# Last attention group taken by sequences, and the token masks built in the first group

## The chip, the cores and the metric

The kernel runs on 1 core of one Trainium2 chip. The metric is the device time of one execution in microseconds (us): 590.84 us, the median of 3 runs (588.93 to 592.22).

## The reference, cut to what matters

One decoder layer on x of shape 4 sequences x 256 tokens x 256 channels, all float32:

```python
x = x + attn(layernorm(x))              # 16 heads of 128, mxfp4-style codes * scales as weights
h = layernorm(x)                        # routed FFN: 4 experts, all with weights ctx[e] (256 x 256)
expert_ids = min(clip(token_ids, 0, 12499) // 3125, 3)
for e in range(4):
    g = silu(h @ ctx[e].T); u = h @ ctx[e].T
    y = (g * u) @ ctx[e].T
    out = where(expert_ids == e, y, out)
x = x + out
x = x + moe(layernorm(x))               # 32 experts, top 4 of a sigmoid router, and a shared expert
```

The masks of this case are the four tests `expert_ids == e` for 1024 tokens, as numbers 0 and 1 on all 128 partitions.

## The kernel before, in words

Tokens are 1024 = 8 row tiles of 128. Float32 products are made of three passes over a high and a low part (`mm3`, L723 to L725). The 16 heads are taken two at a time in G = 8 groups; a group has PAIRS = 8 pairs of (head of the group `hp`, sequence `b`), in the order (0,0) (0,1) (0,2) (0,3) (1,0) (1,1) (1,2) (1,3). The body of a group (`body`, run by `over_groups`: group 0, a loop for groups 1 to 6, group 7) is a software pipeline of slots. In slot i TensorE makes the scores of pair i, then a projection tile of place 0, the transposes (`turn`) of pair i-2, the product with V (`attend`) of pair i-3, and a tile of place 1. Which tiles stand where is the table `slot_tiles`: "qk" tiles of the second head, "v" tiles, "w" tiles (output projection of the group before, one for each sequence, added to the residual `x_acc` by VectorE, L1232), and "next" tiles (first head of the next group). Group 7 has no "next" tiles; its own four output projections stood in slots 8 to 11.

ScalarE does exp (L1098), the high parts of every tile (L1075, L1082), of the transposed probabilities (`pT_hi`, L1110) and of the attention output (`oT_hi`, L1119). VectorE does the row maximum (L1260), its negative (`nmax`, L1264), the scaling of the probabilities (L1273) and the low parts (L1241, L1245, L1281, L1288). Every engine works its own queue strictly in the order written.

GpSimd (POOL) prepares the weights, four chunks for each group (H0, VC, H1, WC): `prep` multiplies codes by scales (L524, counted by `p_wm`), waits until ScalarE has made the high part (`weights_high`, L1052, counted by `a_wh`), and makes the low part (L527, counted by `p_wl`). In groups 1 to 6 ScalarE makes the high part of H0 at the end of slot 1, of VC in slot 5, H1 in slot 6 and WC in slot 7, and its `wait(act, p_wm, count)` stands in its queue ahead of the exp of the next slot. `masks()` (L545 to L555) stood at the head of group 7 in the queue of GpSimd: 4 comparisons and 2 subtractions over 1024 columns. The token ids had landed in group 0. In group 0 the same queue ends with the prep of WC and `constants()`.

After group 7 comes the layer norm of the first token half (statistics, variances, square root on ScalarE, reciprocals with a Newton step, rows; L653 to L682), its transposes on TensorE (L702), high and low parts (L708, L714), then the routed FFN: 16 steps, `pre(n)` and `post(n)` on TensorE, silu on ScalarE (L1149), multiplication with the mask on GpSimd (L591) and the rest on VectorE. `pre(0)` waits for the low parts of the first half. The transposes of the second half stand behind `pre(2)`. Then follow the router and the 32 experts in 8 trips of 8 tiles.

Of the kernel before, what the change touches and what calls it, by code (L numbers as in the profile page):

```python
# [17 lines left out]
P = 128  # L18
T = 1024
# [14 lines left out]
NH = T // HALF  # L34
NE, TOPK, FI = 32, 4, 128
# [29 lines left out]

def slot_tiles(first, last):

    s = [[("qk", Q, 1, 0), ("w", W, 0, 0)],  # L70
         [("qk", K, 1, 0), ("w", W, 0, 1)],
         [("qk", Q, 1, 1), ("v", V, 0, 0)],
         [("v", V, 0, 1), ("w", W, 0, 2)],
         [("v", V, 0, 2), ("qk", K, 1, 1)],
         [("v", V, 0, 3), ("w", W, 0, 3)],
         [("next", Q, 0, 0), ("next", K, 0, 0)],
         [("next", Q, 0, 1), ("next", K, 0, 1)]]
    def tile(t):
        if first and t[0] == "w":
            return ("ctx", None, 0, t[3])  # L80
        return None if last and t[0] == "next" else t
    return [[tile(t) for t in slot] for slot in s]
# [10 lines left out]
class Plan:  # L93
# [3 lines left out]
    def __init__(self, g):  # L97
        self.g = g
        self.first = isinstance(g, int) and g == 0
        self.last = isinstance(g, int) and g == G - 1  # L100
        self.slots = slot_tiles(self.first, self.last)
        n = 0
        self.tiles = []
        start = 4 + 16 * g
        for i, slot in enumerate(self.slots):
            for place, t in enumerate(slot):
                if t is not None:
                    self.tiles.append((i, t, start + n, n, place))
                    n += 1
        if self.last:  # L110
            for b in range(B):
                self.tiles.append((PAIRS + b, ("w", W, 0, b), start + n, n, 1))
                n += 1

    def of_slot(self, i, place):
        if i < 0:
            return [] if self.first else [(("prev", K, 0, 1), None, 1, False)]
        return [(t, number, pos, s >= PAIRS) for s, t, number, pos, at in self.tiles if s == i and at == place]
# [21 lines left out]
    def freed(self, pos):  # L140

        if pos >= 2:
            t = self.tiles[pos - 2][1]
            final = self.last and self.tiles[pos - 2][0] >= PAIRS
        else:
            t, final = ("prev", (Q, K)[pos], 0, 1), False
        kind, m, hp, n = t
        if kind in ("prev", "qk", "next"):
            return "qk", self.qk_count(t)
        if kind == "v":  # L150
            return "v", self.v_count(n)
        if kind == "ctx":
            return "ctx", n + 1
        return "w", self.w_done_count(n, final)

    def w_tile_number(self, b):

        for s, t, number, pos, place in self.tiles:
            if t[0] == "w" and t[3] == b and s < PAIRS:
# [18 lines left out]
def decoder_layer(nc, a, out):  # L178
    ctx = ExitStack()
    with ctx:  # L180
# [78 lines left out]
        mask = sb("mask", [P, NROUTE, T])  # L259
# [252 lines left out]
        def _(pool):  # L512
# [16 lines left out]
            for n, nm in enumerate(("bq", "bk", "bv")):  # L529
# [5 lines left out]
                               base=0, pattern=[[-1, P]], channel_multiplier=1).then_inc(p_const, 1)  # L535
            for n, c in enumerate((H0, H1, VC)):
# [9 lines left out]
            def masks():  # L546
# [3 lines left out]
                for e in range(NROUTE):  # L550
                    pool.tensor_scalar(mask[:, e, :], ids[:, :], float(per * e) if e else float(per), None,
                                       ALU.is_ge if e else ALU.is_lt).then_inc(p_mask, 1)
                pool.wait_ge(p_mask, NROUTE)
                for e in range(1, NROUTE - 1):
                    pool.tensor_tensor(mask[:, e, :], mask[:, e, :], mask[:, e + 1, :], ALU.subtract).then_inc(p_mask, 1)  # L555
# [16 lines left out]
            def body(pl):  # L572
                g = pl.g
                if pl.last:
                    masks()
                for c in ((WC,) if pl.last else (H0, VC, H1, WC)):
# [4 lines left out]
                    if pl.first and c == WC:  # L581
                        constants()

# [3 lines left out]
            pool.wait_ge(p_mask, 2 * NROUTE - 2)  # L587
# [132 lines left out]
        def _(pe):  # L720
# [14 lines left out]
            def proj_tile(pl, tile, number, pos, final=False):  # L735
# [31 lines left out]
                else:  # L767
# [3 lines left out]
                    wait(pe, v_o, pl.pair(PAIRS if final else 0) - B + n + 1)  # L771
# [9 lines left out]
            def scores(pl, i):  # L781
                p = pl.pair(i)
                wait(pe, a_exp, p - 1 if not (pl.first and i < 2) else 0)
                hp, b = i // B, i % B
# [20 lines left out]
            def attend(pl, i):  # L805
# [4 lines left out]
                hp, b = (i % PAIRS) // B, i % B  # L810
                if 0 <= i < B:
# [13 lines left out]
            def body(pl):  # L825
                for i in range(PAIRS + (DRAIN + 1 if pl.last else 0)):
# [45 lines left out]
            ln_tensor(pe, 1, 0, ENDS[0])  # L872
# [173 lines left out]
        def _(act):  # L1046
# [44 lines left out]
            def body(pl):  # L1091
                for i in range(PAIRS + (DRAIN + 1 if pl.last else 0)):
# [18 lines left out]
                    if not (pl.first and i < ATTEND) and i < PAIRS + ATTEND:  # L1111
                        j = i - ATTEND
                        hp, b = (j % PAIRS) // B, j % B
# [10 lines left out]
                    if (i in prep_slots and not pl.last) or (i == PAIRS - 2 and pl.last):  # L1124
# [4 lines left out]
                        elif c != WC or not pl.first:  # L1129
                            kind = {VC: "v", H1: "qk", WC: "w"}[c]  # L1130
                            wait(act, t_j, [tile[2] for tile in pl.tiles if tile[1][0] == kind and tile[0] < PAIRS][-1] + 1)
                        weights_high(c, pl.weights(c, 0 if c == WC else 1))

            over_groups(act, body)

            ln_scalar(act, 1, 0)
# [72 lines left out]
        def _(dve):  # L1209
# [45 lines left out]
            def body(pl):  # L1255
                for i in range(PAIRS + (DRAIN + 2 if pl.last else 0)):
# [26 lines left out]
                    if not (pl.first and i < ATTEND) and i < PAIRS + ATTEND:  # L1283
                        j = i - ATTEND
                        hp, b = (j % PAIRS) // B, j % B
# [4 lines left out]
                                                 op0=ALU.add, op1=ALU.subtract).then_inc(v_o, 1)  # L1290
                    if pl.last and i == PAIRS + 2:
# [8 lines left out]
            ln_low(dve, 1, 0, ENDS[0])  # L1300
# [185 lines left out]
```

## Time and profile before

| what | value |
|---|---|
| median of the runs shown | 590.84 us |
| profiled execution | 591.11 us, span 589.4 us |
| granted TensorE clock, mean of the span | 0.935 |
| PE busy | 511.3 us (87%) |
| DVE busy | 426.6 us (72%) |
| ACT busy | 288.2 us (49%) |
| POOL busy | 233.5 us (40%) |

Attention fills the span from about 28 us to 348 us, the routed FFN the stretch from 354 to about 406 us, the router and the experts the rest. PE, DVE, ACT and POOL are TensorE, VectorE, ScalarE and GpSimd. One group in the loop takes 38.92 us.

### The profile page before, as it was taken

To read this page: it belongs to the slowest core of one execution; us is meant where nothing else is said; L and a number is where in the kernel's file an instruction comes from. 1 tells how busy PE (TensorE), PEld (TensorE's weight loads), DVE (VectorE), ACT (ScalarE), POOL (GpSimd) and SP (SyncE) were. 2 spreads that over 40 slices of the span, in tenths; PEclk is the share of its full clock that TensorE was granted. 3 is DMA by queue.
4 is the path that set the end of the run, shared out by engine and by line. 5 is a ranking of instruction groups with operands and counts; after the bars stand their busy time and mean duration, and the time that the engine had idled before them with its cause. 6 is when DMAs were issued, how large, how long until landed. Compare 5 with 4: busy or idle time off the path is not lost.

```text
span 589.4 us, 11588 instructions
## 1 busy us (share of the span) xinstructions
PE 511.3 (87%) x3291; PEld 453.0 (77%) x3292; DVE 426.6 (72%) x967; ACT 288.2 (49%) x785; POOL 233.5 (40%) x221
## 2 busy tenths in 40 slices
PE   5899999999999999999997679997837999999800
PEld 5688898998998989989887677886625888888600
DVE  5689988989889888898899776568685444444542
ACT  2466656556666666566654625444400444444400
POOL 4307413313123042131384004445005666777773
PEclk9789999999999999999999888999875999999955
DMA  7252211202102122020072009991101455423642
GB/s 214 65 138 55 63 29 51 65 1 83 32 27 62 27 53 62 14 75 0 0 237 86 2 2 296 296 264 37 36 2 35 136 156 147 134 82 112 193 135 89
DMA packets 60893, 52.91 MB, mean 90 GB/s; under 512 B 5545, under 2 KB 58623, under 8 KB 60800
## 3 DMA queue, kind: packets, MB, share of 16 engines
q1 hardware_dynamic: 55752, 43.90, 25.3%
q0 software_dynamic: 4704, 8.44, 5.8%
q8 instruction: 16, 0.26, 0.2%
q10 hardware_dynamic: 408, 0.20, 0.1%
q14 instruction: 13, 0.11, 0.1%
HBM read 46.21 MB, written 14.68 MB: 103 GB/s over the span
## 4 chain that ended last, share of the span: by engine, by line
PE 54%; DVE 19%; issue 9%; POOL 9%; ACT 4%; DMA 3%; POOLq 1%; DVEq 0%; ACTq 0%
PE bank L723 14%; PE bank L724 13%; PE bank L725 13%; PE bank L893 5%; POOL yg L639 5%; POOL xg_last L628 3%; DVE qk_lo L1245 3%; PE bank L801 3%; DVE rmax L1260 3%; DVE nmax L1264 3%; PE bank L901 2%; ACT qk_hi L1082 2%; DMA x_in<-in_x 2%; ACT prob L1098 1%; DVE pT_lo L1281 1%
## 5 line engine op out<-in xcount | busy, mean ns | idle before, releaser
L527 POOL TENSOR_TENSOR w_lo<-st_c,w_hi 128x512 fp32r<-128x512 f32 x32 | 41.2, 1287 | 220.7 <-ACT w_hi L1052 220.7
L1098 ACT ACTIVATE prob<-bank,nmax 128x256 f32<-128x256 f32 x128 | 59.5, 470 | 111.2 <-DVE nmax L1264 111.2
L893 PE MATMUL bank<-moe_w,xT 128*128 x256 | 67.6, 388 | 0.0
L723 PE MATMUL bank<-hT_hi,w_lo 128*128 128x512 f32 x128 | 53.9, 421 | 7.8 <-DVE qk_lo L1245 4.2
L1340 DVE TENSOR_TENSOR hid<-bank,sg 128x128 f32<-128x128 f32 x72 | 20.9, 291 | 53.4 <-ACT sg L1164 52.7
L1245 DVE SCALAR_TENSOR_TENSOR qk_lo<-bank,b_col,qk_hi 128x512 fp32r<-128x512 f32 x64 | 47.8, 747 | 13.2 <-ACT qk_hi L1082 12.2
L1260 DVE TENSOR_REDUCE rmax<-bank 128x2 f32<-128x512 f32 x64 | 43.9, 686 | 15.8 <-PE bank L725 15.2
L1164 ACT ACTIVATE sg<-bank 128x128 f32<-128x128 f32 x72 | 19.8, 277 | 70.0 <-PE bank L893 69.9
L1273 DVE TENSOR_SCALAR prob<-prob,rinv 128x256 f32<-128x256 f32 x128 | 52.0, 448 | 2.3
L724 PE MATMUL bank<-hT_lo,w_hi 128*128 128x512 f32 x128 | 51.6, 403 | 0.0
L725 PE MATMUL bank<-hT_hi,w_hi 128*128 128x512 f32 x128 | 51.4, 402 | 0.0
L1082 ACT ACTIVATE qk_hi<-bank,b_col 128x512 fp32r<-128x512 f32 x64 | 44.0, 687 | 10.8 <-PE bank L725 10.0
L893 PEld LDWEIGHTS bank<-moe_w,xT 128*128 128x128 f32 x256 | 44.8, 195 | 3.6
L1281 DVE TENSOR_TENSOR pT_lo<-bank,pT_hi 128x512 fp32r<-128x512 f32 x64 | 43.6, 681 | 3.1 <-ACT pT_hi L1110 3.1
L723 PE MATMUL bank<-pT_hi,v_lo 128*128 128x256 f32 x128 | 41.8, 326 | 4.0 <-DVE pT_lo L1281 2.7
L524 POOL TENSOR_TENSOR st_c<-st_c,st_s 128x512 f32<-128x512 f32 x32 | 40.9, 1279 | 5.5 <-DMA st_s<-in_wq_scales 5.5
L801 PE MATMUL bank<-ident,prob 128*128 128x128 f32 x256 | 38.6, 274 | 1.8 <-DVE prob L1273 1.8
L723 PE MATMUL bank<-w_hi,oT_lo 128*128 128x256 f32 x128 | 37.4, 292 | 2.4 <-DVE qk_lo L1245 2.4
L1110 ACT CAST pT_hi<-bank 128x512 fp32r<-128x512 f32 x64 | 38.1, 595 | 2.6 <-PE bank L801 2.6
L591 POOL TENSOR_TENSOR x_in<-x_in,mask 128x512 f32<-128x512 f32 x16 | 20.9, 1306 | 45.0 <-ACT x_in L1149 45.0
L901 PE MATMUL bank<-moe_w,hidT 128*128 x128 | 38.3, 382 | 0.0
L723 PE MATMUL bank<-w_hi,hT_lo 128*128 128x256 f32 x128 | 36.3, 283 | 2.0 <-DVE qk_lo L1245 2.0
(187 smaller groups left out, 1609.0 us busy)
## 6 DMA issues: line engine op xcount, KB each, us to landing
y_dram<-ysb SPq DMA_DIRECT2D x64, 128.0 KB, 2.4
moe_w<-in_w_gate SPq DMA_DIRECT2D x8, 512.0 KB, 8.5
moe_w<-in_w_up SPq DMA_DIRECT2D x8, 512.0 KB, 7.2
moe_w<-in_w_down SPq DMA_DIRECT2D x4, 1024.0 KB, 8.8
st_c<-in_wq_codes SPq DMA_DIRECT2D x16, 128.0 KB
st_c<-in_wv_codes SPq DMA_DIRECT2D x8, 256.0 KB
st_c<-in_wo_codes SPq DMA_DIRECT2D x8, 256.0 KB
st_s<-in_wo_scales SPq DMA_DIRECT2D x16, 128.0 KB
```

The costliest lines, as they stand in the source:

```text
L723: pe.matmul(o, l_lo, r_hi, start=start, stop=False, skip_group_check=share)
L724: pe.matmul(o, l_hi, r_lo, start=False, stop=False, skip_group_check=share)
L725: return pe.matmul(o, l_hi, r_hi, start=False, stop=stop, skip_group_check=share)
L801: mm = pe.transpose(bP[i % 2][:, kt * S + qt * P:kt * S + qt * P + P], prob[:, i % 4, qt, kt * P:kt * P + P], ident[:, :])
L893: mm = pe.matmul(bG[n % 2][:, 0:2 * FI], xT_of(kt), w, start=kt == 0, stop=kt == KT - 1)
L901: pe.matmul(bY[n % 2][:, 0:D], hidT[:, n % 2, :], w, start=True, stop=True).then_inc(t_dn, 1)
L1082: act.activation(qk_hi[:, hp, m, n * HALF:(n + 1) * HALF], src[:, :], ACT.Identity, bias=b_col[:, bass.ds(g_h + m * H, 1)]).then_inc(a_qk, 1)
L1098: ex = act.activation(prob[:, i % 4, qt, :], bS[i % 2][:, qt * S:(qt + 1) * S], ACT.Exp, bias=nmax[:, i % 2, qt:qt + 1], scale=SCALE, accu ...
L1245: dve.scalar_tensor_tensor(out=qk_lo[:, hp, m, n * HALF:(n + 1) * HALF], in0=src[:, :], scalar=b_col[:, bass.ds(g_h + m * H, 1)], in1=qk_h ...
L1260: dve.tensor_reduce(rmax[:, i % 2, :], bS[i % 2][:, :].rearrange("p (q k) -> p q k", q=2), AX.X, ALU.max).then_inc(v_m1, 1)
L1273: sc = dve.tensor_scalar(prob[:, j % 4, qt, :], prob[:, j % 4, qt, :], rinv[:, j % 2, qt:qt + 1], None, ALU.mult)
L1281: dve.tensor_tensor(pT_lo[:, j % 2, :, :].rearrange("p a b -> p (a b)"), bP[j % 2][:, :], pT_hi[:, j % 2, :, :].rearrange("p a b -> p (a b ...
```

## The change

Four edits. In group 7 the pairs are taken in the order of `LAST_ORDER`; the tiles stand in other slots, with the output projections of sequences 0 and 1 in slots 6 and 7 and those of 2 and 3 in slots 10 and 11; the high part of the last WC chunk is made in slot 5 instead of 6. The layer norm of the first half is spread over slots 8 to 11, its transposes standing ahead of the last output projection. The masks are bf16, built in pieces of 256 columns (16 comparisons, 8 subtractions) behind `constants()` in group 0. A tile `beyond` of 4096 bf16 columns is added behind `mask` and cleared by GpSimd ahead of its first `prep`.

```diff
+LAST_ORDER = [(0, 0), (0, 1), (1, 0), (1, 1), (0, 2), (0, 3), (1, 2), (1, 3)]
 def slot_tiles(first, last):
+    if last:
+        return [[("qk", Q, 1, 0), ("w", W, 0, 0)],
+                [("qk", K, 1, 0), ("w", W, 0, 1)],
+                [("qk", Q, 1, 1), ("v", V, 0, 0)],
+                [("v", V, 0, 1), ("w", W, 0, 2)],
+                [("qk", K, 1, 1), ("w", W, 0, 3)],
+                [("v", V, 0, 2), None],
+                [("v", V, 0, 3), ("w", W, 1, 0)],
+                [None, ("w", W, 1, 1)]]
...
-            for b in range(B):
-                self.tiles.append((PAIRS + b, ("w", W, 0, b), start + n, n, 1))
+            for i, b in ((PAIRS + 2, 2), (PAIRS + 3, 3)):
+                self.tiles.append((i, ("w", W, 1, b), start + n, n, 1))
...
-        mask = sb("mask", [P, NROUTE, T])
+        mask = sb("mask", [P, NROUTE, T], BF16)
+        beyond = sb("beyond", [P, NROUTE, T], BF16)
...
+            pool.memset(beyond[:, :, :], 0.0)
             for n, c in enumerate((H0, H1, VC)):
                 prep(c, n + 1, 16 * DMAS[c])
...
+                for i in range(MASK_PIECES):
+                    sl = slice(i * S, (i + 1) * S)
+                    for e in range(NROUTE):
+                        pool.tensor_scalar(mask[:, e, sl], ids[:, sl], float(per * e) if e else float(per), None,
+                                           ALU.is_ge if e else ALU.is_lt).then_inc(p_mask, 1)
+                    pool.wait_ge(p_mask, i * MASK_STEPS + NROUTE)
+                    for e in range(1, NROUTE - 1):
+                        pool.tensor_tensor(mask[:, e, sl], mask[:, e, sl], mask[:, e + 1, sl], ALU.subtract).then_inc(p_mask, 1)
...
             def body(pl):
                 g = pl.g
-                if pl.last:
-                    masks()
...
                     if pl.first and c == WC:
                         constants()
+                        masks()
...
# TensorE, slots of the last group
+                    if pl.last and i == PAIRS + 3:
+                        ln_tensor(pe, 1, 0, ENDS[0])
                     for tile in pl.of_slot(i, 1):
                         proj_tile(pl, *tile)
...
# ScalarE
-                    if (i in prep_slots and not pl.last) or (i == PAIRS - 2 and pl.last):
+                    if (i in prep_slots and not pl.last) or (i == PAIRS - 3 and pl.last):
...
+                    if pl.last and i == PAIRS + 1:
+                        ln_scalar(act, 1, 0)
...
# VectorE
+                    if pl.last and i == PAIRS:
+                        dve.wait_ge(v_w, 4 * G - 1)
+                        statistics()
+                    if pl.last and i == PAIRS + 1:
+                        variances()
                     if pl.last and i == PAIRS + 2:
-                        dve.wait_ge(v_w, 4 * G - 1)
-                        for part in ln_vector(dve, 1, 0, x_acc):
-                            part()
+                        reciprocals()
+                        rows()
+                    if pl.last and i == PAIRS + 3:
+                        ln_low(dve, 1, 0, ENDS[0])
```

## Rows read from the trace of the kernel before

**Rows 1.** The page: the clock granted to TensorE in 40 slices, in tenths.
```profile
PEclk9789999999999999999999888999875999999955
```

**Rows 2.** Busy time by stretch: stretch, its us, each engine, granted clock, DMA share, GB/s.
```profile
298.00:318.00 20.00, 16.45 (x122) 15.08 (x121) 19.36 (x33) 9.69 (x29) 17.66 (x8) 1.00 0.69 237
```

**Rows 3.** The tile mask, instructions that write it: count, ns min/median/max, starts, forms.
```profile
L551 POOL TENSOR_SCALAR mask<-ids x4: 2770/2774/2799, 298.7 to 307.2; 128x1024 f32<-128x1024 int32 x4
L555 POOL TENSOR_TENSOR mask<-mask x2: 2373/2404/2435, 310.1 to 312.4; 128x1024 f32<-128x1024 f32 x2
```

**Rows 4.** Timeline of DVE, group 7: start us, us, instruction.
```profile
309.00 3.62 DVE L1273 TENSOR_SCALAR prob<-prob,rinv 128x256 f32<-128x256 f32 x2
...
316.80 0.62 DVE L1273 TENSOR_SCALAR prob<-prob,rinv 128x256 f32<-128x256 f32 x2
```

**Rows 5.** Timeline of PE: first matmul of slots 0 and 5, groups 6 and 7.
```profile
256.74 0.28 PE L723 MATMUL bank<-qk_hi,qk_lo 128*128 128x256 f32 x1
...
280.90 0.28 PE L723 MATMUL bank<-qk_hi,qk_lo 128*128 128x256 f32 x1
...
295.67 0.28 PE L723 MATMUL bank<-qk_hi,qk_lo 128*128 128x256 f32 x1
...
323.76 0.28 PE L723 MATMUL bank<-qk_hi,qk_lo 128*128 128x256 f32 x1
```

**Rows 6.** Timeline of POOL, start of the program and groups 0 and 1.
```profile
3.05 0.23 POOL L531 MEMSET ident<- 128x128 f32 x1
...
3.63 0.29 POOL L534 TENSOR_SCALAR_AFFINE_SELECT ident<-ident 128x128 f32<-128x128 f32 x1 [0.24 <-POOL zeros L532]
9.41 1.28 POOL L524 TENSOR_TENSOR st_c<-st_c,st_s 128x512 f32<-128x512 f32 x1 [5.49 <-DMA st_s<-in_wq_scales]
...
44.63 5.71 POOL L543 TENSOR_TENSOR x_acc<-x_in,bo_b 128x256 f32<-128x256 f32 x8
...
65.37 0.29 POOL L567 TENSOR_SCALAR_AFFINE_SELECT before<-ones 128x128 bf16<-128x128 bf16 x1
...
65.90 1.28 POOL L524 TENSOR_TENSOR st_c<-st_c,st_s 128x512 f32<-128x512 f32 x1
```

**Rows 7.** Timeline of ACT, group 1, end of slot 1 and slot 2.
```profile
72.14 0.64 ACT L1052 CAST w_hi<-st_c 128x512 fp32r<-128x512 f32 x1
74.28 0.47 ACT L1098 ACTIVATE prob<-bank,nmax 128x256 f32<-128x256 f32 x1 [1.50 <-DVE nmax L1264]
...
75.19 0.69 ACT L1082 ACTIVATE qk_hi<-bank,b_col 128x512 fp32r<-128x512 f32 x1
```

**Rows 8.** Timeline of PE, group 1, slot 3: first v matmul, and the turn behind it.
```profile
77.55 0.28 PE L723 MATMUL bank<-w_hi,hT_lo 128*128 128x256 f32 x1
...
78.97 0.60 PE L801 MATMUL bank<-ident,prob 128*128 128x128 f32 x4
```

**Rows 9.** Timeline of PE, group 7, slots 8 and 9, and routed stage.
```profile
337.97 0.58 PE L723 MATMUL bank<-pT_hi,v_lo 128*128 128x256 f32 x1 [2.38 <-DVE pT_lo L1281]
...
341.98 0.79 PE L801 MATMUL bank<-ident,prob 128*128 128x128 f32 x4
...
353.76 0.80 PE L723 MATMUL bank<-hT_hi,cT_lo 128*128 128x512 f32 x1 [1.75 <-DVE hT_lo L714]
```

**Rows 10.** Timeline of ACT and then of DVE, end of group 7.
```profile
335.23 1.28 ACT L694 ACT_TABLE_LOAD   x1
...
346.24 0.48 DVE L1288 SCALAR_TENSOR_TENSOR oT_lo<-bank,b_col,oT_hi 128x256 fp32r<-128x256 f32 x1 [0.60 <-ACT oT_hi L1119]
346.64 1.40 DVE L653 BATCH_NORM_STATS2 bn<-x_acc 128x6 f32<-128x256 f32 x4
...
348.79 0.18 DVE L665 RECIPROCAL rstd<-sd 128x4 f32<-128x4 f32 x1 [0.27 <-ACT sd L690]
...
349.80 1.38 DVE L682 TENSOR_SCALAR h_row<-x_acc,mv,rstd 128x256 f32<-128x256 f32 x4
351.10 1.28 DVE L1232 TENSOR_TENSOR x_acc<-bank,x_acc 128x512 f32<-128x512 f32 x2
```

More of the change, by code:

```diff
@@ L34 @@
 NH = T // HALF
+MASK_PIECES, MASK_STEPS = T // S, 2 * 4 - 2
 NE, TOPK, FI = 32, 4, 128
@@ L80, in tile @@
             return ("ctx", None, 0, t[3])
-        return None if last and t[0] == "next" else t
+        return t
     return [[tile(t) for t in slot] for slot in s]
@@ L110, in __init__, with pair_of @@
         if self.last:
-            for b in range(B):
-                self.tiles.append((PAIRS + b, ("w", W, 0, b), start + n, n, 1))
+            for i, b in ((PAIRS + 2, 2), (PAIRS + 3, 3)):
+                self.tiles.append((i, ("w", W, 1, b), start + n, n, 1))
                 n += 1
+    def pair_of(self, i):
+        if self.last and 0 <= i < PAIRS:
+            return LAST_ORDER[i]
+        return i % PAIRS // B, i % B
     def of_slot(self, i, place):
@@ L117, in of_slot @@
             return [] if self.first else [(("prev", K, 0, 1), None, 1, False)]
-        return [(t, number, pos, s >= PAIRS) for s, t, number, pos, at in self.tiles if s == i and at == place]
+        return [(t, number, pos, t[0] == "w" and t[2] == 1) for s, t, number, pos, at in self.tiles if s == i and at == place]
     def pair(self, i):
@@ L143, in freed @@
             t = self.tiles[pos - 2][1]
-            final = self.last and self.tiles[pos - 2][0] >= PAIRS
+            final = t[0] == "w" and t[2] == 1
         else:
@@ L158, in w_tile_number @@
         for s, t, number, pos, place in self.tiles:
-            if t[0] == "w" and t[3] == b and s < PAIRS:
+            if t[0] == "w" and t[3] == b and t[2] == 0:
                 return number
@@ L770, in proj_tile @@
                         wait(pe, p_wl, pl.weights(WC, 0) if final else (pl.g - 1) * 4 + 3 + 4)
-                    wait(pe, v_o, pl.pair(PAIRS if final else 0) - B + n + 1)
+                    wait(pe, v_o, pl.pair(LAST_ORDER.index((1, n)) if final else n - B) + 1)
                     for i in range(2):
@@ L809, in attend @@
                 wait(pe, v_o, p - 1 if not (pl.first and 0 <= i < 2) else 0)
-                hp, b = (i % PAIRS) // B, i % B
-                if 0 <= i < B:
+                hp, b = pl.pair_of(i)
+                if hp == 0 and 0 <= i < PAIRS:
                     wait(pe, v_v, pl.v_count(b))
@@ L1130, in body @@
                             kind = {VC: "v", H1: "qk", WC: "w"}[c]
-                            wait(act, t_j, [tile[2] for tile in pl.tiles if tile[1][0] == kind and tile[0] < PAIRS][-1] + 1)
+                            wait(act, t_j, [tile[2] for tile in pl.tiles if tile[1][0] == kind and
+                                            not (kind == "w" and tile[1][2] == 1)][-1] + 1)
                         weights_high(c, pl.weights(c, 0 if c == WC else 1))
+                    if pl.last and i == PAIRS + 1:
+                        ln_scalar(act, 1, 0)
             over_groups(act, body)
-            ln_scalar(act, 1, 0)
             ln_high(act, 1, 0, ENDS[0])
@@ L1290, in body @@
                                                  op0=ALU.add, op1=ALU.subtract).then_inc(v_o, 1)
+                    if pl.last and i >= PAIRS:
+                        statistics, variances, reciprocals, rows = ln_vector(dve, 1, 0, x_acc)
+                    if pl.last and i == PAIRS:
[3 more added lines that the diff above has]
+                        variances()
                     if pl.last and i == PAIRS + 2:
-                        dve.wait_ge(v_w, 4 * G - 1)
-                        for part in ln_vector(dve, 1, 0, x_acc):
-                            part()
+                        reciprocals()
+                        rows()
+                    if pl.last and i == PAIRS + 3:
+                        ln_low(dve, 1, 0, ENDS[0])
             over_groups(dve, body)
```

16 lines of the change are left out of this document (4 added, 12 removed).

## Prediction

> **What bounds the kernel now.** I read the page first. Its clock line shows TensorE at 9 tenths or more nearly everywhere but in a dip in slices 23 to 25 (324 to 368 us; a slice is 589.4/40 = 14.7 us) and in the router stage behind it [rows 1]. The busy time by stretch gives the size of a first hole, the timelines that of a second. Between 298 and 318 us TensorE works 16.45 of 20 us while POOL works 17.66 us and VectorE 19.36 us [rows 2]. The first hole is the masks: 4 comparisons of 2.77 us and 2 subtractions of 2.40 us fill POOL [rows 3], and two probability scalings on VectorE that take 0.62 us together when POOL is quiet take 3.62 us under them [rows 4]. The second hole is the drain of attention: TensorE waits 2.38 us for a low part at 337.97, and from the last low part of attention at 346.24 to the routed stage at 353.76 a layer norm runs through VectorE, piece by piece [rows 9, 10]. Everywhere else in attention TensorE is the bound, with ScalarE and VectorE only a little behind it, so a stall of either passes to TensorE after about one slot.
>
> **The masks leave group 7.** The price is read from the slot starts. From slot 0 to slot 5 group 6 takes 280.90 - 256.74 = 24.16 us, group 7 takes 323.76 - 295.67 = 28.09 us [rows 5], with the same tiles. So 3.9 us go. Bounds: 3.5 us (the hole of rows 2, 20 - 16.45) and 4.3 us. What was behind the masks on POOL, the scaling of the last WC chunk, has its user in slot 5 and is early.
>
> **How long the masks take in group 0.** They start behind `constants()`, where the product of group 1's H0 starts now, at 65.90 us [rows 6]. Additions of 256 columns take 5.71/8 = 0.71 us apiece [rows 6]; four of them make 2.86 us where one subtraction of 1024 takes 2.40 [rows 3], so an extra piece costs (2.86 - 2.40)/3 = 0.15 us. A comparison of 1024 takes 2.77 us, four pieces 2.77 + 3 x 0.15 = 3.2 us. Sum: 4 x 3.2 + 8 x 0.71 = 12.9 + 5.7 = 18.6 us, and with four waits on its own semaphore, estimated at 0.1 us each from the 0.24 us that POOL idles ahead of its first select [rows 6], M = 19.0 us. The bf16 type may alter this. No row shows it for these operations; the nearest is a select of 128 columns, 0.29 us in f32 and 0.29 us in bf16 [rows 6]. I take no effect. Bounds: half of it, 9.5 us, if the time went by bytes written, and 24 us if conversion cost a quarter more.
>
> The Trainium skill speaks for a shorter M. "GPSIMD Engine Reference", section 3.1, gives 1.03 to about 1.8 cycles at 1.2 GHz for an element of an instruction with one input and about 2.6 with two. By it a comparison piece is at most 0.38 us and a subtraction piece 0.56 us, M = 16 x 0.38 + 8 x 0.56 = 10.6 us. The trace disagrees on the comparisons (2.77 us for 1024 int32 columns is 3.2 cycles each) and about agrees on the subtractions (2.40 us is 2.8 cycles).
>
> **Who waits for it.** Queued behind the masks on POOL is the product of H0 for group 2 (1.28 us). ScalarE makes the high part of it at the end of slot 1, at 72.14 us [rows 7], and its queue holds the exp of slot 2 behind that wait. Before, the product was done at 67.18, 5.0 us early. Now it is done at 65.90 + 19.0 + 1.3 = 86.2 us, so ScalarE stands for 14.1 us. TensorE goes on through slot 2 and the scores of slot 3, since their inputs were made ahead. The v tile of slot 3, at 77.55 us [rows 8], needs the bank that the Q tile of slot 2 used, and that needs ScalarE and VectorE behind the wait: high part 0.64, exp of two halves 0.9 (74.28 to 75.19), the Q high part 0.69 [rows 7], the low part about 0.75, hand-overs 0.1: 3.1 us. The v tile starts at 89.3 instead of 77.55: 11.8 us lost; as a formula, M - 7.2 us. Nothing makes it up, since from there TensorE is again the bound. In this stretch VectorE is also held by POOL pieces (0.7 to 0.8 us instead of 2.8 per scaling), but it is late for nothing that the stall doesn't cover. Bounds: 2.3 us (M = 9.5) and 17 us (M = 24).
>
> **The clock behind the stall.** After its waits in the drain TensorE runs slowly: 18 matmuls of 256 columns take 341.98 - 337.97 = 4.0 us [rows 9], where 12 take 1.42 us at full clock [rows 8], 18 thus 2.1 us. That is the lower level, 1.2 GHz, and costs 1.9 us. I add 2.0 us behind the stall in group 1; bounds 0 and 2.7.
>
> **The clearing of `beyond`.** 128 columns of f32 take 0.23 us [rows 6]. At (0.23 - 0.10)/128 = 1.0 ns each, 0.10 an estimated fixed part, 4096 columns take 4.2 us, from 3.9 to 8.1 us. POOL waits for a DMA until 9.41 us [rows 6], which hides it there. VectorE does its small layer norm operations at 6.2 us and can be held until 8.1 us, which I let through as 0.4 us; TensorE's warming matmuls cover the rest. Bounds: 0, and 4 us at 2.35 ns a column (2.40/1024, [rows 3]).
>
> **The drain.** Slots 5, 6 and 7 now hold two projections that stood in slots 8 and 9; they fill time in which TensorE waited. By the order of the queues, slot 5 takes 3.4 us (one tile), slot 6 4.9 us (two), both estimates from the 4.8 us mean of slots 0 to 4 with two tiles (24.16/5, [rows 5]) less one tile of 1.42 us [rows 8]. The scores of pair 7 then start 8.3 us behind the start of slot 5, and exp, the table load of 1.28 us [rows 10], which stays where it was, transposes, the V product and their parts follow. In this chain the projection ahead of the transposes of pair 7 (12 slow matmuls of the 18 above, 2.6 us) goes, and the four statistics (1.3 us) come in ahead of a low part. I count 20.3 us to the last low part oT_lo; it was 346.24 - 323.76 = 22.5 us [rows 5, 10]. That is 2.2 us.
>
> Behind it, before: 353.76 - 346.24 = 7.5 us to `pre(0)` [rows 9, 10]. After: oT_lo 0.4, reciprocals 1.0 (348.79 to 349.80) and rows 1.4 [rows 10], transposes 0.9 behind the last row, the last projection 2.6 at the slow clock, the router transposes 0.3: 6.6 us, limited by TensorE and not by the low parts. The statistics and variances (348.79 - 346.64 = 2.15 us) and one of two additions (0.64) go from this chain, and the projection on TensorE takes most of it back. That is 0.9 us. Together 3.1 us. Bounds: 1.5 us if the slots are held by VectorE, and 5.5 us if TensorE keeps its full clock. The second half's rows come at about 4.5 us behind its last addition, as before, and `pre(0)` to `pre(2)` cover them.
>
> **Sum**, on the profiled execution: 591.1 - 3.9 - 3.1 + 11.8 + 2.0 + 0.4 = 598.3 us. It lies 0.3 us above the median of the runs shown, so the forecast for the median is 598.0 us. The 1.7 us outside the span is unchanged.
>
> **Rivals.** *Short masks* (other side). Everything hangs on M: gains of 7.0 us meet costs of M - 7.2 + 2.4 us, so it decides at M = 11.8 us; below, the change is faster. With M = 9.5 to 10.6 the stall is 2.3 to 3.4 us, the clock stays up, and the time is 590.8 - 7.0 + 2.9 + 0.4 = 587.1 us. For it: the skill's rule above, and that bf16 is half the bytes; against it: the equal selects and the comparisons' own 2.77 us. *Cancelling*: M near 13 us with 1 to 2 us of slow clock, or a larger gain in the drain; 590.8 + 5.8 + 1.5 + 0.4 - 7.5 = 591 us. *Hold by both*: POOL and VectorE delay one another piece by piece, 24 contacts of 0.2 us, M = 24 us: 598 + 5 = 603 us. For it: rows 4; against: six mask instructions took 16.2 us from first to last, hardly above their sum of 15.9. *The drain gives nothing*: the order changes, but the chain through the table load and VectorE keeps its length; 598 + 3.1 = 601 us.
>
> **How the numbers follow.** Forecast 0.59 (own range 594 to 601), drain without gain 0.10, hold by both 0.06, cancelling 0.08, short masks 0.17. Range for 8 in 10: 588 to 602. About 0.5% (3 us) is what a measurement of this kernel tells from no change. Faster 0.17, within 0.08, slower 0.75.
>
> **What would show it.** In the trace after: 24 mask instructions from about 66 us on, the comparisons near 0.8 us; the high part of H0 in group 1 at 86 us, released by POOL's product; TensorE idle some 12 us ahead of the v tile of slot 3, with the granted clock down behind it; slots 0 to 5 of group 7 in 24.2 us; 22.5 us less 2.2 from slot 5 to the last oT_lo. Comparisons of a third of a microsecond would prove it wrong.

## The result, and the profile after

The kernel after takes 594.83 us (median of 9 runs, 593.19 to 598.71), the kernel before 590.84 us (9 runs, 587.34 to 592.22). The ratio is 1.0094, with a 95% interval of 1.0068 to 1.012: the change costs 4.0 to 7.1 us. The profiled execution after took 593.46 us. Every event below is read from one profiled execution of its kernel, so it carries that execution's own variations.

The page after, beside the same lines of before (span 589.4 us, [rows 1]):

```profile
span 591.6 us, 11606 instructions
...
PE 509.2 (86%) x3291; PEld 451.2 (76%) x3292; DVE 422.3 (71%) x967; ACT 287.8 (49%) x785; POOL 236.4 (40%) x240
...
PEclk9899978999999999999999989999885999999955
```

Busy times have hardly moved, so the loss is waiting. The 7 and the 8 in the clock line (the sixth and seventh slice, from 74 to 104 us) are new; before they were 9 and 9. The busy time by stretch (columns as in [rows 2]) shows it. First the kernel after:

```profile
62.00:78.00 16.00, 13.41 (x99) 12.26 (x97) 11.26 (x23) 4.90 (x14) 14.78 (x26) 1.00 0.13 38
78.00:95.00 17.00, 5.99 (x33) 6.00 (x34) 5.45 (x12) 6.11 (x16) 10.02 (x12) 0.60 0.09 23
```

Then the kernel before:

```profile
62.00:78.00 16.00, 15.61 (x113) 14.28 (x112) 15.19 (x31) 9.74 (x26) 6.21 (x13) 1.00 0.25 67
78.00:95.00 17.00, 17.00 (x131) 16.23 (x130) 14.38 (x33) 9.56 (x28) 2.53 (x2) 1.00 0.10 25
```

TensorE goes from 17.00 busy us in 17 to 5.99, and its granted clock from 1.00 to 0.60. POOL, whose work used to lie in the shadow, is full first. What it does there, by the instructions that write the tile mask (columns as in [rows 3]):

```profile
L574 POOL TENSOR_SCALAR mask<-ids x16: 846/849/875, 64.4 to 82.6; 128x256 bf16<-128x256 int32 x16
...
L578 POOL TENSOR_TENSOR mask<-mask x8: 666/669/723, 68.1 to 84.1; 128x256 bf16<-128x256 bf16 x8
```

The waits of 64 to 95 us name who stood behind it (waiting engine and tile, then who released it: us in total, times, longest):

```profile
ACT w_hi L1075 <- POOL st_c L544: 16.0, 1, 16.0
DVE qk_lo L1270 <- ACT qk_hi L1105: 14.6, 2, 14.1
PE bank L745 <- DVE qk_lo L1270: 13.6, 2, 13.2
```

One long wait is handed from engine to engine. The chain of waits (start, us, engine, tile, line) gives the same story in order of time: masks, the product of H0, ScalarE's queue behind it, a low part, TensorE.

```profile
64.36 0.88 POOL mask L574
...
84.13 0.67 POOL mask L578
84.80 1.23 POOL st_c L544
...
86.94 0.65 ACT prob L1121 x3
87.59 0.59 ACT qk_hi L1105
88.20 0.76 DVE qk_lo L1270
89.01 0.58 PE bank L745
```

The timeline of PE after has the milestones that answer to [rows 5, 8, 9]: the v tile of slot 3 in group 1, the scores of slot 4, slots 0 and 5 of group 7, and `pre(0)`.

```profile
89.01 0.58 PE L745 MATMUL bank<-w_hi,hT_lo 128*128 128x256 f32 x1 [13.23 <-DVE qk_lo L1270]
...
95.16 0.28 PE L745 MATMUL bank<-qk_hi,qk_lo 128*128 128x256 f32 x1
...
309.27 0.28 PE L745 MATMUL bank<-qk_hi,qk_lo 128*128 128x256 f32 x1
...
333.31 0.28 PE L745 MATMUL bank<-qk_hi,qk_lo 128*128 128x256 f32 x1
...
359.45 0.47 PE L745 MATMUL bank<-hT_hi,cT_lo 128*128 128x512 f32 x1
```

The last low part of attention, from the timeline of DVE after (before: 346.24, [rows 10]):

```profile
354.19 0.49 DVE L1313 SCALAR_TENSOR_TENSOR oT_lo<-bank,b_col,oT_hi 128x256 fp32r<-128x256 f32 x1 [1.32 <-ACT oT_hi L1142]
```

Subtracting neighbours gives the whole account, in the profiled executions. "Shift" is how much later the event comes after than before.

| event | before | after | shift | what this step adds |
|---|---|---|---|---|
| w_lo of WC, group 0 (where the masks start) | 63.44 | 61.79 | -1.65 | start of the program -1.65 |
| v tile of slot 3, group 1 | 77.55 | 89.01 | +11.46 | stall +13.1 |
| slot 4, group 1 | 81.59 | 95.16 | +13.57 | slow clock +2.1 |
| slot 0, group 7 | 295.67 | 309.27 | +13.60 | 0.0 in the groups between |
| slot 5, group 7 | 323.76 | 333.31 | +9.55 | masks gone -4.05 |
| last oT_lo | 346.24 | 354.19 | +7.95 | drain -1.6 |
| pre(0) | 353.76 | 359.45 | +5.69 | layer norm -2.3 |
| first product of the shared expert | 406.67 | 410.93 | +4.26 | routed stage -1.4 |
| last four products of the experts | 556.30 | 560.16 | +3.86 | router and experts -0.4 |
| end of the span | 589.4 | 591.6 | +2.2 | the end behind the experts -1.7 |

Behind the experts the kernel only gathers and adds their results, with the same instructions in both kernels, and took 1.7 us less in this execution; nothing here says why. The medians differ by 4.0 us, the lower end of the interval, and the interval holds the 4.26 us of the shared expert's row. That sum has at least 1.65 us of luck in it: the start of the program was early for a reason that is not the change, as the last section shows. Without it the account gives 5.9 us, which the interval holds too.

### The profile page after: what moved, and what is told of

Read it like the earlier page. It is cut to its first block, busy times and chain, and to the rows that moved or that the text cites. A ratio compares the mean times of both kernels' runs of the same rounds, so it can differ in the third digit from the quotient of the medians.

```text
span 591.6 us, 11606 instructions
## 1 busy us (share of the span) xinstructions
PE 509.2 (86%) x3291; PEld 451.2 (76%) x3292; DVE 422.3 (71%) x967; ACT 287.8 (49%) x785; POOL 236.4 (40%) x240
## 2 busy tenths in 40 slices
DMA packets 60893, 52.91 MB, mean 89 GB/s; under 512 B 5545, under 2 KB 58623, under 8 KB 60800
## 4 chain that ended last, share of the span: by engine, by line
PE 49%; DVE 20%; POOL 12%; issue 9%; ACT 6%; DMA 2%; POOLq 1%; DVEq 0%; ACTq 0%
PE bank L745 12%; PE bank L746 11%; PE bank L747 11%; PE bank L916 5%; POOL yg L661 5%; POOL xg_last L650 3%; DVE rmax L1285 3%; DVE nmax L1289 3%; DVE qk_lo L1270 3%; PE bank L823 3%; POOL mask L574 2%; PE bank L924 2%; ACT prob L1121 2%; ACT qk_hi L1105 2%; DVE pT_lo L1306 2%
## 5 line engine op out<-in xcount | busy, mean ns | idle before, releaser
L1105 ACT ACTIVATE qk_hi<-bank,b_col 128x512 fp32r<-128x512 f32 x64 | 44.0, 688 | 10.4 <-PE bank L747 8.1
L1298 DVE TENSOR_SCALAR prob<-prob,rinv 128x256 f32<-128x256 f32 x128 | 47.2, 410 | 2.3
L745 PE MATMUL bank<-w_hi,hT_lo 128*128 128x256 f32 x128 | 36.7, 287 | 13.2 <-DVE qk_lo L1270 13.2
L640 POOL DMA_INDIRECT xg<-h_dram,src x32 | 32.1, 1005 | 13.8 <-issue 7.0
```

Source lines behind the costliest of these rows:

```text
L745: pe.matmul(o, l_lo, r_hi, start=start, stop=False, skip_group_check=share)
L1105: act.activation(qk_hi[:, hp, m, n * HALF:(n + 1) * HALF], src[:, :], ACT.Identity, bias=b_col[:, bass.ds(g_h + m * H, 1)]).then_inc(a_qk, 1)
L1298: sc = dve.tensor_scalar(prob[:, j % 4, qt, :], prob[:, j % 4, qt, :], rinv[:, j % 2, qt:qt + 1], None, ALU.mult)
```

## The experiments

All ran on other chips, eight on a second one and three (the kernel after again, only the cutting, everything that pays) on a third. The kernel before takes 665.64 and 665.36 us in the two batches on the second and 659.1 us on the third, 68 to 75 us more than on the first; the time goes behind the start of the shared expert. Attention runs there as on the first chip, so each ratio is against the kernel before in the same batch, and events are compared up to the first product of the shared expert. Gains and losses of whole kernels in us are worked out from the ratio and that kernel before. Edits are shown against the kernel after where nothing else is said. The events of all kernels stand in one table behind them.

**The kernel after, again.** No edit; it ties the chips together.

> The changed kernel as it is, beside the kernel before on the chip of the other experiments, where all kernels spend some 65 us more in the expert trips. The stretches of attention should be as on the first chip (13 us stall, 24.0 us for slots 0 to 5 of group 7), and the difference in time +4 us, the ratio 1.006 here.

668.31 us, ratio 1.011 (1.0069 to 1.015), 7.2 us. The stall is there again, 13.23 us ahead of the v tile, and the intervals of the ratios on the two chips overlap. The slow clock behind the stall cost 1.4 us in this execution where it cost 2.1 in the first.

**Masks back at the head of group 7**, as bf16 pieces.

```diff
                 g = pl.g
+                if pl.last:
+                    masks()
...
                         constants()
-                        masks()
```

> The changed kernel with the 24 mask pieces (bf16, 256 columns) moved from group 0 back to the head of group 7 on GpSimd. Stall theory (the cost of the change is GpSimd's queue holding the product of H0 behind the masks, 13.1 us of TensorE idle and 2.1 us of slow clock behind it): group 1 has no idle stretch, the high part of H0 comes about 5 us behind its product, and the time falls by 15.2 us less what the pieces cost VectorE in group 7, 0 to 4 us, to 580 to 584 us. Rival (VectorE is held by GpSimd's pieces wherever they run, and that is the price): the loss moves with them to group 7, slots 0 to 5 take 10 us or more above 24.1 us, and the time stays at 592 to 596 us.

656.49 us, ratio 0.9858 (0.9814 to 0.9902). The stall is gone (slot 4 of group 1 at 81.77), as expected. But group 7 did not get its 3.9 us back: with all 24 pieces in it, its slots 0 to 5 take 24.22 us.

```profile
295.67 0.28 PE L746 MATMUL bank<-qk_hi,qk_lo 128*128 128x256 f32 x1
...
319.89 0.28 PE L746 MATMUL bank<-qk_hi,qk_lo 128*128 128x256 f32 x1
```

In the busy time by stretch of this kernel POOL is busier than in [rows 2], and TensorE works 19.82 us instead of 16.45:

```profile
298.00:318.00 20.00, 19.82 (x149) 18.50 (x148) 18.77 (x40) 11.02 (x32) 18.37 (x24) 1.00 0.71 238
```

So the type, the length of the pieces or the new order took the cost away. The next runs tell these apart.

**Only the cutting**: the kernel before, f32 masks at the head of group 7, in pieces of 256 columns.

```diff
# against the kernel before
-                for e in range(NROUTE):
-                    pool.tensor_scalar(mask[:, e, :], ids[:, :], ...)
+                for i in range(MASK_PIECES):
+                    sl = slice(i * S, (i + 1) * S)
+                    for e in range(NROUTE):
+                        pool.tensor_scalar(mask[:, e, sl], ids[:, sl], ...)
...
```

> The kernel before with one edit: its masks at the head of group 7, in float32, are built in 256-column pieces instead of 1024-column ones. Theory (it is the length of one GpSimd instruction that VectorE's scalings wait for, not the work as a whole): the scalings take at most 0.9 us more, slots 0 to 5 of group 7 take 24.2 us instead of 28.1 us, and the time falls by 3.5 to 4 us, the ratio is 0.994. Rival (in the kernel with masks back in group 7 the other tile order was what hid them): slots 0 to 5 keep 26 to 28 us and the time moves by less than 2 us.

655.57 us, ratio 0.9936 (0.9914 to 0.9958). This one edit gains 4.2 us, with f32 masks and the old order. Slots 0 to 5 of group 7 take 24.03 us. The pair of scalings that took 3.62 us in [rows 4] takes at most 1.36:

```profile
295.26 0.28 PE L726 MATMUL bank<-qk_hi,qk_lo 128*128 128x256 f32 x1
...
319.29 0.28 PE L726 MATMUL bank<-qk_hi,qk_lo 128*128 128x256 f32 x1
```

```profile
307.68 1.36 DVE L1276 TENSOR_SCALAR prob<-prob,rinv 128x256 f32<-128x256 f32 x2
```

The timeline of the kernel before shows what the pair of 3.62 us waited for. Its first scaling took 1.16 us and ended at 310.16, just behind the last comparison (310.01). The second ended at 312.62, just behind the first subtraction (312.46):

```profile
309.00 1.16 DVE L1273 TENSOR_SCALAR prob<-prob,rinv 128x256 f32<-128x256 f32 x1
```

```profile
310.09 2.37 POOL L555 TENSOR_TENSOR mask<-mask 128x1024 f32<-128x1024 f32 x1
```

**The type alone**: the kernel after with an f32 mask and without `beyond`.

```diff
-        mask = sb("mask", [P, NROUTE, T], BF16)
-        beyond = sb("beyond", [P, NROUTE, T], BF16)
+        mask = sb("mask", [P, NROUTE, T])
...
-            pool.memset(beyond[:, :, :], 0.0)
```

> The changed kernel with the mask tile in float32 again, 256-column pieces in group 0 as before this edit, and without beyond and its clearing. If the type has no part in it: comparisons 0.85 us and subtractions near 0.71 us, the same stall of 13 us within 0.5 us. VectorE's small operations of the first layer norm are no longer held at 6 us, its rows come 1.0 us earlier, which moves the start of group 1 by 0 to 1 us. Rival (bf16 made the pieces shorter, or makes the routed multiplication of 1.17 us instead of 1.30 us pay): comparisons above 0.95 us, stall 15 us, and the routed stage 1 us or more longer.

671.8 us, ratio 1.0114 (1.0066 to 1.0162), as the kernel after. The tile mask in this kernel:

```profile
L572 POOL TENSOR_SCALAR mask<-ids x16: 846/850/877, 63.8 to 82.4; 128x256 f32<-128x256 int32 x16
L611 POOL TENSOR_TENSOR x_in<-x_in,mask x16: 1289/1301/1433, 364.1 to 402.9; 128x512 f32<-128x512 f32 x16
L576 POOL TENSOR_TENSOR mask<-mask x8: 722/730/796, 67.5 to 84.0; 128x256 f32<-128x256 f32 x8
```

A comparison takes 850 ns in f32 and 849 in bf16. A subtraction takes 730 against 669, the multiplication of the routed stage 1301 against 1168, which is hidden (from `pre(0)` to the shared expert 51.59 us against 51.48). The type is worth 8 x 0.06 = 0.5 us of mask time, which the stall shows (13.73 us against 13.23), and nothing elsewhere.

**The masks' move alone**, on the kernel before: bf16 pieces behind `constants()`, and `beyond`.

```diff
# against the kernel before; masks in pieces as in the kernel after
+            pool.memset(beyond[:, :, :], 0.0)
...
-                if pl.last:
-                    masks()
...
                         constants()
+                        masks()
```

> The kernel before with nothing but the masks moved: bf16 pieces in group 0, tile beyond and its clearing included; order of pairs, tiles and layer norm as before. Stall theory: +15.2 us in group 1, -4.0 us in group 7, so 590.8 + 11.2 = 602 us; the reordering is then worth 602 - 595 = 7 us. Rival (reordering gives less than the trace suggests, since the routed stage takes it back): 597 to 599 us.

678.0 us, ratio 1.0192 (1.0146 to 1.0238). The stall of the kernel after, without its drain:

```profile
88.94 0.58 PE L727 MATMUL bank<-w_hi,hT_lo 128*128 128x256 f32 x1 [13.25 <-DVE qk_lo L1249]
```

**Half of the masks in group 0**, the other half at the head of group 7. M is halved, and the stall should follow M - 7.3 us, the prediction's formula with its constant read again from the kernel after.

```diff
+                if pl.last:
+                    masks((2, 3))
...
-                        masks()
+                        masks((0, 1))
```

> The changed kernel with the first two of the four mask pieces in group 0 and the other two at the head of group 7. The masks then hold GpSimd for 10.2 us instead of 20.4 at the start of group 1. Stall theory, with the slack read from the changed kernel (stall of TensorE = length of the masks less 7.3 us): TensorE waits 2.9 us instead of 13.2 us ahead of the v tile of slot 3 and keeps its clock, so group 1 is 12.3 us shorter than in the changed kernel; time about 6 us below the kernel before on the same chip. Rival (the stall is contention, in proportion to the pieces): half the loss, 6.6 us, and about 3 us below the kernel before.

661.71 us, ratio 0.9939 (0.9914 to 0.9963). The timeline of PE, group 1:

```profile
81.08 0.58 PE L747 MATMUL bank<-w_hi,hT_lo 128*128 128x256 f32 x1 [3.06 <-DVE qk_lo L1272]
...
83.81 1.06 PE L825 MATMUL bank<-ident,prob 128*128 128x128 f32 x4
...
87.88 0.28 PE L747 MATMUL bank<-qk_hi,qk_lo 128*128 128x256 f32 x1
```

The wait of 3.06 us is what the formula gives. That the clock would stay up was wrong: from the v tile to slot 4 the kernel needs 6.80 us where before needs 4.04 ([rows 8] to 81.59), so 2.8 us more, nearly as much as the wait itself. Four transposes take 1.06 us where they take 0.60 at full clock [rows 8]. The two pieces in group 7 cost it a little as well: its slots 0 to 5 take 24.67 us.

**One piece in each of groups 1 to 4**, between the parts of H0 and of VC, where POOL has time (its loop over the groups is written out for this).

```diff
-                for i in range(MASK_PIECES):
...
+                    if c == H0 and isinstance(g, int) and 1 <= g <= MASK_PIECES:
+                        masks(g - 1)
                     if pl.first and c == WC:
                         constants()
-                        masks()
```

> The changed kernel with one mask piece (4 comparisons and 2 subtractions of 256 columns, 5.1 us) in each of groups 1 to 4, between the prep of H0 and that of VC, where GpSimd idles for 15 to 16 us; its loop is peeled for that, the instructions are the same 24. Stall theory: no stall, slack stays 10 us, all 15.2 us come back, and the contention with VectorE costs under 1 us for a piece: 579 to 582 us. Rival (contention is the price): each piece costs 2 to 3 us of TensorE time in its group, 588 to 592 us in all.

656.14 us, ratio 0.9861 (0.9823 to 0.99). Neither group 1 (39.27 us) nor group 7 (24.05 us for slots 0 to 5) pays. Groups 2 to 6 take 195.71 us together where the kernel before takes 194.62: some 1 us. This kernel does no better than the one with the pieces at the head of group 7.

**No masks.** The comparisons and subtractions are left out.

```diff
+            pool.memset(mask[:, :, :], 1.0).then_inc(p_mask, 1)
...
-                        masks()
```

> The changed kernel without the 24 mask instructions; the mask tile is set to 1 once, by a GpSimd memset of 4096 bf16 columns behind that of beyond, so every expert is added for every token (the token masks are left out). Stall theory: this is the floor, 579 to 580 us, and the version with spread masks lies within 2 us of it. Rival: it lies 8 us or more below the spread version. A second memset of 3.5 us at the start may delay the first weights by 1 to 2 us.

660.23 us, ratio 0.9933 (0.9907 to 0.996), slower than the two kernels above that build them where they don't stall. The masks' place comes at 65.93 us, 4.3 later than in the kernel with spread masks. The second clearing is part of that: it holds a small VectorE operation for 4.73 us where one clearing holds it for 1.25. The rest is the clock granted early in the program, 0.69 in this execution and 0.83 in that one (last section). Kernels with one clearing and 0.66 to 0.69 have the place at 63.62 to 64.16, so of the 4.3 us each has about 2. How the difference of the medians divides is not shown. From the masks' place to the shared expert it takes 333.36 us, against 333.88 with the pieces in group 7 and 335.07 with them spread. So pieces in group 7 cost 0.5 us of what could be had.

**The order without the spread layer norm**: the kernel with spread masks, its layer norm in one block as before.

```diff
# against the kernel with spread masks
-                    if pl.last and i == PAIRS + 3:
-                        ln_tensor(pe, 1, 0, ENDS[0])
...
+            ln_tensor(pe, 1, 0, ENDS[0])
...
-                    if pl.last and i == PAIRS:
-                        dve.wait_ge(v_w, 4 * G - 1)
-                        statistics()
-                    if pl.last and i == PAIRS + 1:
-                        variances()
                     if pl.last and i == PAIRS + 2:
-                        reciprocals()
-                        rows()
...
+                        dve.wait_ge(v_w, 4 * G - 1)
+                        for part in ln_vector(dve, 1, 0, x_acc):
+                            part()
```

> The version with spread masks, with the order of the pairs and the places of the tiles as in the change, but the layer norm of the first half in one block in slot 10 and its transposes, square root and low parts behind the group, as in the kernel before. If the order of pairs and the earlier projections are what shortens the drain: from slot 5 of group 7 to the last oT_lo 19.6 us (20.9 less the statistics that stood in between), to the first routed matmul about 27.1 us against 26.1 us, so the spread of the layer norm is worth 1 us and the order 2.9 us. Rival (the spread of the layer norm is what counts): 29 to 30 us to the first routed matmul.

657.25 us, ratio 0.9892 (0.9849 to 0.9935). The last low part comes 19.38 us behind slot 5, and `pre(0)` 27.09 us; with the layer norm spread it is 20.89 and 26.15. So the spread makes the low part 1.5 us later and `pre(0)` 0.9 us earlier. To the shared expert it is worth 1.4 us; the new order is worth 3.9 (82.91 us from slot 5 to there before, 79.02 here; 83.32 and 83.57 in the two other kernels with the old order, by which it would be 4.3 and more).

**The table load one slot later**, behind the first `pT_hi` of slot 8.

```diff
# against the kernel with spread masks
-                        if pl.last and i == PAIRS - 1:
-                            fetch_table(act, ACT.Sqrt)
...
+                    if pl.last and i == PAIRS:
+                        fetch_table(act, ACT.Sqrt)
```

> The version with spread masks, with the load of the square root table moved from behind the last exp (slot 7) to slot 8, behind the high part of the probabilities of pair 6, where ScalarE idled for 1.1 us. If the table load stands in the chain of the drain: the last oT_lo comes 1.0 to 1.5 us earlier, and so do the routed stage and the end: 578 to 581 us by the first chip, 1 to 1.5 us below the version with spread masks. Rival (VectorE or TensorE takes over at once): under 0.3 us.

654.0 us, ratio 0.9841 (0.9806 to 0.9876). The timeline of ACT in this kernel:

```profile
331.49 0.59 ACT L1137 CAST pT_hi<-bank 128x512 fp32r<-128x512 f32 x1 [0.17 <-PE bank L829]
332.09 1.28 ACT L722 ACT_TABLE_LOAD   x1
```

From slot 5 to the last low part it takes 19.42 us instead of 20.89, and to the shared expert 76.14 instead of 77.63. In the kernel after, the load (344.59 to 345.87) stands ahead of that `pT_hi` and of the one before it, on the chain of the last pairs. The ratios of this kernel and of the one with spread masks, 0.9841 and 0.9861, lie within each other's intervals; the 1.5 us are read from the traces alone.

**Everything that pays**: the same with f32 masks, without `beyond` and its clearing.

> The version with spread masks and the later table load, with float32 masks and without beyond and its clearing. The multiplications with the mask take 1.30 us instead of 1.17 us, hidden in the routed stage; VectorE's first layer norm is 1 us earlier. Theory: 0 to 1 us below the version with the later table load, ratio 0.983. Rival (the first layer norm isn't what sets the start, or the multiplications come to light): the same or 0.5 us above.

650.03 us, ratio 0.9842 (0.9804 to 0.988): 10.4 us faster than the kernel before, where the kernel after in the same batch is 7.2 us slower. The kernel above had 0.9841 in its batch, so the gain lies in the pieces, the order, the spread layer norm and the table load. What f32 masks and leaving `beyond` out add can't be told from the ratios; the traces have the masks' place 0.7 us earlier and 0.5 us less from slot 5 to the shared expert.

| kernel | masks' place | slot 4, g1 | slot 0, g7 | slot 5, g7 | last oT_lo | pre(0) | shared expert |
|---|---|---|---|---|---|---|---|
| after, again | 64.16 | 96.77 | 310.85 | 334.89 | 355.78 | 361.03 | 412.51 |
| masks back | 63.62 | 81.77 | 295.67 | 319.89 | 340.78 | 346.04 | 397.50 |
| only the cutting | 62.92 | 81.07 | 295.26 | 319.29 | 342.05 | 349.57 | 402.61 |
| type alone | 61.19 | 95.08 | 309.16 | 333.20 | 354.08 | 359.34 | 410.93 |
| move alone | 61.72 | 95.00 | 309.12 | 333.14 | 356.05 | 363.57 | 416.71 |
| half | 64.03 | 87.88 | 301.94 | 326.61 | 347.48 | 352.73 | 404.19 |
| spread | 61.64 | 79.86 | 295.03 | 319.08 | 339.97 | 345.23 | 396.71 |
| no masks | 65.93 | 84.10 | 298.31 | 322.36 | 342.57 | 347.82 | 399.29 |
| order only | 61.32 | 79.52 | 294.56 | 318.61 | 337.99 | 345.70 | 397.63 |
| table later | 61.89 | 80.12 | 295.15 | 319.20 | 338.62 | 343.88 | 395.34 |
| all that pays | 61.16 | 79.45 | 294.26 | 318.31 | 337.12 | 342.38 | 393.96 |

## Why the prediction was right, step by step

The side and the mechanism held: the masks hold the product of H0, ScalarE waits for it, TensorE stands, and the clock falls behind. The size came out near the lower end: 598.0 us forecast (own range 594 to 601), 594.83 measured. The four rivals fell. Terms of the sum, forecast against measured:

- *M*, the length of the masks: 19.0 against 20.4 us (64.36 to 84.80). The comparison was estimated at 0.8 us and took 0.85, start to start 0.93. "I take no effect" of the type: right for the comparisons, to 1 ns. The rival *short masks* fails on one row: a comparison took 849 ns. So does the estimate of 10.6 us that the prediction took from the Trainium skill ("GPSIMD Engine Reference", section 3.1). Its "at most 0.38 us" read 1.8 cycles as a ceiling, while the page calls them the best case. *Hold by both* fails on M too (20.4, not 24), *the drain gives nothing* on the -5.3, *cancelling* on the 13.1, although the larger gain in the drain that it allowed for did come.
- *Stall*: 11.8 us forecast, 13.1 measured; only M was mis-sized. The formula M - 7.2 gives 13.2 for the measured M, and TensorE waited 13.23. With half of the masks (M = 10.2) the wait was 3.06 us, so the formula holds at a second point. The high part of H0 came at 86.03 us, almost the forecast 86.2: the longer masks and the earlier start cancelled there, which is luck.
- *Slow clock*: +2.0 against +2.1, and 1.4 us in the other execution of the same kernel. A match to 0.1 us is partly luck.
- *Masks leave group 7*: -3.9 against -4.05. The size was read rightly, but it was booked to the wrong edit. The prediction gave it to the masks leaving group 7, although it wrote that pieces hold a scaling for 0.7 to 0.8 us instead of 2.8. The cut alone gives the same gain with the masks still there and POOL as busy as before, so what cost TensorE time was the length of one GpSimd instruction of 1024 columns. The change paid 15 us in group 0 for something that cutting alone had already bought.
- *`beyond`*: +0.4. The clearing took 3.51 us and held VectorE's first small operations (1.25 us for one that takes 0.17 in the f32 kernel). At the early clock of 0.83 the masks' place is at 61.32 to 61.89 us with it and at 61.16 and 61.19 without, so it costs about 0.5 us. The -1.65 in the account comes from elsewhere, see below.
- *Drain*: -3.1 against -5.3, the largest miss of the change's own terms, though inside its bounds. The sum was +7.2 and came out as +4.3: the drain gave 2.2 more, the start 2.05 more (1.65 of it luck), and the stall took 1.3 back. The part to the last low part was -2.2 against -1.6: behind the scores of pair 7 the chain took 12.85 us where 12.0 were forecast. The table load, whose move in an experiment gave 1.5 us, and the statistics stand in it. The part behind it was -0.9 against -2.3, and nothing was forecast for the routed stage, which gained 1.4. Most of these two misses is the clock. The prediction let the last projection run slowly in 2.6 us. TensorE, at work without a pause from 351.93 us on, was back at full clock from 357.6 us on, and the projection took 1.6. The routed stage then starts at full clock. Before:

```profile
346.20:353.80 7.60, 4.26 (x31) 3.32 (x29) 7.05 (x24) 1.29 (x4) 0.00 (x0) 0.92 0.02 4
353.80:370.00 16.20, 16.20 (x78) 12.98 (x79) 10.57 (x29) 8.52 (x15) 6.61 (x5) 0.83 1.14 297
```

After:

```profile
354.20:359.40 5.20, 5.20 (x32) 4.30 (x30) 4.58 (x14) 1.07 (x2) 0.00 (x0) 0.79 0.00 0
359.40:375.00 15.60, 14.71 (x84) 12.04 (x84) 11.42 (x30) 8.08 (x15) 6.68 (x6) 1.00 1.00 264
```

The granted clock behind `pre(0)` goes from 0.83 to 1.00. `pre(0)` itself, twelve matmuls, takes 5.42 us before and 2.93 after. Of these 2.5 us the routed stage keeps 1.4, since TensorE now waits 0.89 us for VectorE ahead of its next products. The kernel with the new order but the layer norm in one block stands between the two: it waits 1.40 us ahead of `pre(0)`, makes it in 4.54 us and reaches the shared expert after 51.93 us (52.91 before, 51.48 after). A clock that falls behind a wait was in the prediction as a loss in group 1; that a drain without a wait at its end gives it back was missed.

The sum with all measured terms, to the first product of the shared expert: -1.65 + 13.1 + 2.1 - 4.05 - 5.3 = +4.2, against +4.26 in the account.

## What to carry to other kernels

Before work is moved out of the way of another engine, cut it: the same GpSimd work in instructions a quarter as long cost TensorE next to nothing here, and the move to a place that looked empty put 20 us ahead of a product with 5 us to spare. Price a stall of TensorE with the clock behind it, and look whether a stall removed gives that clock back in the stage behind, as it did here.

## What the runs showed of the hardware that was not expected

- A short wait can cost its own length again. After 3.06 us without work, TensorE's next 4 us of matmuls took 6.8. After 13.2 us it cost 2.1 in one execution of the kernel after and 1.4 in another. So the price did not grow with the wait, and it is not the same each time.
- A VectorE operation can be held beside GpSimd's work whatever its size, until the GpSimd instruction under way ends. In the kernel with cut f32 masks a negation of 2 columns, 0.17 us at other places of the same group, took 1.08 us. The masks start only at 298.25; what ran beside it was GpSimd's low part of a weight chunk, and the two ended at 298.17 and 298.15:

```profile
297.09 1.08 DVE L1267 TENSOR_SCALAR nmax<-rmax 128x2 f32<-128x2 f32 x1
```

```profile
296.87 1.28 POOL L528 TENSOR_TENSOR w_lo<-st_c,w_hi 128x512 fp32r<-128x512 f32 x1 [2.60 <-ACT w_hi L1055]
```

  In the same way the first layer norm's 1.25 us of the kernel after ended at 7.40, the clearing at 7.38. Comparisons don't hold it throughout. In the kernel before the negation passed in 0.17 us in the middle of one:

```profile
302.63 0.17 DVE L1264 TENSOR_SCALAR nmax<-rmax 128x2 f32<-128x2 f32 x1
```

```profile
301.53 2.78 POOL L551 TENSOR_SCALAR mask<-ids 128x1024 f32<-128x1024 int32 x1
```

- The clock at the start of the program is granted differently from one execution to the next. Between 12 and 22 us it was 0.66 before and 0.83 after:

```profile
12.00:22.00 10.00, 7.00 (x21) 5.12 (x22) 8.22 (x21) 4.48 (x8) 4.48 (x4) 0.66 0.61 184
```

```profile
12.00:22.00 10.00, 6.87 (x24) 4.46 (x25) 8.75 (x22) 5.31 (x10) 4.05 (x4) 0.83 0.62 189
```

  The kernel after itself had 0.69 on the third chip, and its masks' place came at 64.16 instead of 61.79. Of the thirteen profiled executions seven had 0.83 and the place at 61.16 to 61.89; six had 0.66 to 0.69 and the place at 62.92 to 65.93. Both groups hold kernels with and without `beyond`, so nearly all of the -1.65 us is not the change. Why one execution gets the better clock stays open.
- The other two chips need some 70 us more behind attention and the routed stage with the same instructions: from the first product of the shared expert to the end of the span 182.7 us before on the first, 260.3 with the masks back on the second, 254.4 with only the cutting on the third. The matmuls of the experts, grouped by line, in the kernel with the masks back (second chip) and in the kernel after (first chip), busy and mean ns, then idle time ahead and what ended it:

```profile
L917 PE MATMUL bank<-moe_w,xT 128*128 x256 | 76.9, 428 | 32.2 <-issue 27.6 <-DVE xT L1461 4.5
```

```profile
L916 PE MATMUL bank<-moe_w,xT 128*128 x256 | 67.5, 387 | 0.0
```

  27.6 us of the waiting is "issue", a wait for nothing that the profile shows. The granted clock is lower as well, 0.76 against 0.92 from the shared expert to the last product of the experts (masks back, and before on the first chip). The cause is open.
